# Expert tiles: two scatters in flight for neighbouring tiles of one expert, and the second projection two tiles late

## The reference, cut to what matters

```python
scores = xf @ gate_w.T + gate_b + bias                     # 2048 tokens, 8 experts
top_scores, top_idx = jax.lax.top_k(scores, 2)
gates = jax.nn.softmax(top_scores, axis=-1)
h = jax.nn.silu(einsum('td,ehd->teh', xf, w1) + b1)        # 512 -> 352
y = einsum('teh,edh->ted', h, w2) + b2                     # 352 -> 512
out = einsum('ted,te->td', y, comb)                        # comb: the two gates of each token
x = x + out
```

## Time and profile before

| what | value |
|---|---|
| three runs, median (lowest to highest) | 1113.1 us (1109.29 to 1113.27) |
| the profiled execution, its own time | 1108.39 us |
| its span in the profile | 1106.6 us |
| PE busy | 1024.7 us, 93% |
| DVE busy | 808.6 us, 73% |
| POOL busy | 377.5 us, 34% |
| stretch from the first to the last scatter instruction | 880.19 to 1098.41 us |

### The profile page before, as it was taken

One profiled execution on the slowest core, in us unless ns is written; L12 is line 12 of the kernel. 1 busy time (PEld: TensorE's weight loads), 2 busy tenths in 40 slices (PEclk: granted clock), 3 DMA queues, 4 the chain that ended last, 5 costly groups with the idle time before them and its releaser, 6 DMA issues.

```text
span 1106.6 us, 16870 instructions
## 1 busy us (share of the span) xinstructions
PE 1024.7 (93%) x4963; PEld 843.8 (76%) x4964; DVE 808.6 (73%) x1606; ACT 392.4 (35%) x825; POOL 377.5 (34%) x307
## 2 busy tenths in 40 slices
PE   4999899999999997999999999999959899899994
PEld 3888688888888875788888888888748777777773
DVE  6888876687676777789999989999898534443342
ACT  3345444444444554221221221221247533333331
POOL 2665554455454443200000000000047244444442
PEclk9999999999999999999999999999979999999998
DMA  6001620001000121521111111111335154455443
GB/s 238 1 0 38 233 72 20 20 20 37 19 20 20 58 76 57 201 67 38 47 47 47 47 38 38 47 47 38 114 103 202 35 89 88 92 95 91 88 88 55
DMA packets 45551, 76.72 MB, mean 69 GB/s; under 512 B 4072, under 2 KB 16400, under 8 KB 45392
## 3 DMA queue, kind: packets, MB, share of 16 engines
q1 hardware_dynamic: 36784, 55.88, 14.9%
q0 software_dynamic: 8736, 20.45, 10.3%
HBM read 52.99 MB, written 23.33 MB: 69 GB/s over the span
## 4 chain that ended last, share of the span: by engine, by line
PE 67%; DMA 15%; DVE 10%; issue 4%; ACT 2%; POOL 0%; POOLq 0%; SPq 0%; DVEq 0%; ACTq 0%
DMA out<-y,slot_token 13%; PE pK L1383 10%; PE pK L1385 10%; PE pK L1384 10%; PE pX L1383 5%; PE pX L1385 5%; PE pX L1384 5%; PE pA L1383 5%; PE pA L1385 5%; PE pA L1384 5%; PE pA L1497 2%; PE pT L1449 1%; DMA xg<-xn_dram,slot_token 1%; DVE gprod L1182 1%; DVE xn_lo L1018 1%
## 5 line engine op out<-in xcount | busy, mean ns | idle before, releaser
L855 ACT ACTIVATE q<-pK 128x512 f32<-128x512 f32 x64 | 38.3, 599 | 277.1 <-PE pK L1385 277.1
L559 POOL TENSOR_TENSOR kacc<-kacc,k_hi 128x512 f32 (+1 forms) x64 | 91.7, 1433 | 122.0 <-ACT k_hi L733 121.1
L635 POOL TENSOR_TENSOR xb<-x_in,bo_b 128x512 f32<-128x512 f32 x15 | 19.4, 1293 | 319.9 <-DVE x L1168 311.4
L563 POOL TENSOR_TENSOR kacc<-kacc,k_lo 128x512 f32 (+1 forms) x64 | 98.9, 1546 | 34.5 <-DVE k_lo L1040 25.9
L1383 PE MATMUL pA<-k_hi,xn_hi 128*128 128x512 f32 x256 | 101.1, 395 | 7.3 <-DVE k_lo L1040 7.3
L1383 PE MATMUL pX<-m_hi,qsT_hi 128*128 128x512 f32 x256 | 105.7, 413 | 0.0
L647 POOL DMA_INDIRECT out<-y,slot_token x39 | 66.8, 1712 | 113.8 <-DMA out<-y,slot_token 91.9
L1018 DVE TENSOR_TENSOR xn_lo<-xn,xn_hi 128x512 fp32r<-128x512 f32 x64 | 91.1, 1424 | 19.7 <-ACT xn_hi L726 19.7
L1383 PE MATMUL pK<-wq_hi,xnT_hi 128*128 128x512 f32 x256 | 100.9, 394 | 3.1 <-DVE wq_lo L1018 3.1
L1383 PE MATMUL pK<-wk_hi,xnT_hi 128*128 128x512 f32 (+1 forms) x256 | 102.1, 399 | 1.0 <-DVE xnT_lo L1018 1.0
L1384 PE MATMUL pK<-wq_lo,xnT_hi 128*128 128x512 f32 x256 | 100.7, 393 | 0.0
(11 more groups left out here) (232 smaller groups left out, 2460.1 us busy)
## 6 DMA issues: line engine op xcount, KB each, us to landing
w_in<-in_ffn_w SPq DMA_DIRECT2D x22, 256.0 KB, 3.2
w_in<-in_ffn_w SPq DMA_DIRECT2D x8, 704.0 KB, 7.7
xn<-in_attn_hidden_states SPq DMA_DIRECT2D x16, 256.0 KB, 5.8
wk_in<-in_attn_Wk SPq DMA_DIRECT2D x4, 1024.0 KB, 5.1
wv_in<-in_attn_Wv SPq DMA_DIRECT2D x16, 256.0 KB, 2.8
wo_in<-in_attn_Wo SPq DMA_DIRECT2D x16, 256.0 KB, 3.0
wk_in<-in_attn_Wq SPq DMA_DIRECT2D x4, 1024.0 KB, 5.1
xnT_dram<-xnT SPq DMA_DIRECT2D x4, 1024.0 KB, 12.9
```

The lines of the kernel that those rows point to most:

```text
L559: pool.tensor_tensor(acc, acc, f(k_hi[:, b * CW:(b + 1) * CW]), ALU.add).then_inc(pool_own, 1)
L563: pool.tensor_tensor(acc, acc, f(k_lo[:, b * CW:(b + 1) * CW]), ALU.add).then_inc(kacc_done, 1)
L635: pool.tensor_tensor(xb[:, :], x_in[:, :], bo_b[:, :], ALU.add).then_inc(xb_ready, 1)
L855: nc.scalar.activation(q[:, (c % 2) * CW:(c % 2 + 1) * CW], pK[:, (c % 2) * 512:(c % 2 + 1) * 512], ACT.Relu).then_inc(q_ready, 1)
```

## The change

`add_out(i)` now waits for the landing of add_out(i-2) always, and for that of add_out(i-1) only where tile i-1 belongs to another expert or where tile i is filled up entirely. Which it is stands in a new table `add_after`, which DVE works out after `tile_expert`; POOL loads one value of it into a register ahead of each scatter from the fourth on and waits with that. There is one landing semaphore for even and one for odd tiles. Two small POOL instructions put the constants of the table (`add_base`) in an earlier stage.

The second projection runs two tiles late instead of one: PE's loop is h(i), gT(i+1), y(i-2), hT(i). So `hT_hi` and `hT_lo` have two buffers each, DVE's order follows, and POOL gathers five tiles ahead of the scatter instead of three. The work per tile is the same.

```diff
             def add_out(i):
+                if i >= 3:
+                    other = pool.value_load(add_after[0:1, i - 1:i], min_val=16, max_val=16 * NS)
                 pool.wait_ge(y_ready, i + 1)
-                if i > 0:
-                    pool.wait_ge(s_add, 16 * i)
+                if i >= 2:
+                    pool.wait_ge(s_add[i % 2], 16 * (i // 2))
+                if i >= 3:
+                    pool.wait_ge(s_add[1 - i % 2], other)
+                elif i >= 1:
+                    pool.wait_ge(s_add[1 - i % 2], 16)
                 pool.indirect_dma_start(out, bass.IndirectOffsetOnAxis(slot_token[:, i:i + 1].bitcast(U32), 0),
-                                        y[:, i % 2 * D:(i % 2 + 1) * D], None, compute_op=ALU.add).then_inc(s_add, 16)
+                                        y[:, i % 2 * D:(i % 2 + 1) * D], None, compute_op=ALU.add).then_inc(s_add[i % 2], 16)
...
-            gather(2)
+            for i in range(2, 5):
+                gather(i)
             for i in range(NS):
-                if i + 3 < NS:
-                    gather(i + 3)
+                if i + 5 < NS:
+                    gather(i + 5)
                 add_out(i)
...
             link(v.tensor_scalar(tile_expert[:, :], padt[:, 0:TW], float(E - 1), None, ALU.min))
+            link(v.tensor_tensor(same[:, :], padt[:, 1:TW], padt[:, 0:NS], ALU.is_equal))
+            link(v.scalar_tensor_tensor(out=same[:, :], in0=padt[:, 1:TW], scalar=E - 0.5, in1=same[:, :],
+                                        op0=ALU.is_le, op1=ALU.mult))
+            link(v.scalar_tensor_tensor(out=add_after[:, :], in0=same[:, :], scalar=-16.0, in1=add_base[:, :],
+                                        op0=ALU.mult, op1=ALU.add))
...
-            def dve_y(i, b):
+            def dve_y(i, b, added):
                 dve.wait_ge(y_put, i + 1)
                 if not (isinstance(i, int) and i < 2):
-                    dve.wait_ge(s_add, 16 * i - 16)
+                    dve.wait_ge(s_add[b], added)
...
             with dve.Fori(2, NS // 2) as h:
                 for b in range(2):
                     dve_gT(2 * h + (b + 1))
-                    dve_y(2 * h + (b - 1), 1 - b)
-                    dve_hT(2 * h + b)
-            dve_y(NS - 2, 1)
-            dve_hT(NS - 1)
-            dve_y(NS - 1, 0)
+                    dve_y(2 * h + (b - 2), b, 16 * h - 16)
+                    dve_hT(2 * h + b, b)
+            dve_y(NS - 3, 0, 16 * (NS // 2) - 16)
+            dve_hT(NS - 1, 0)
+            dve_y(NS - 2, 1, 16 * (NS // 2) - 16)
+            dve_y(NS - 1, 0, 16 * (NS // 2))
...
             pe_hT(0)
             pe_h(1, first_experts[1])
             pe_gT(2, 0)
-            pe_y(0, first_experts[0])
             pe_hT(1)
             with pe.Fori(1, NS // 2) as h:
                 for b in range(2):
                     i = 2 * h + b
                     pe_h(i, expert(i))
                     pe_gT(2 * h + (b + 1), 1 - b)
-                    pe_y(2 * h + (b - 1), expert(2 * h + (b - 1)))
+                    pe_y(2 * h + (b - 2), b, expert(2 * h + (b - 2)))
                     pe_hT(i)
             pe_h(NS - 1, expert(NS - 1))
-            pe_y(NS - 2, expert(NS - 2))
+            pe_y(NS - 3, 0, expert(NS - 3))
             pe_hT(NS - 1)
-            pe_y(NS - 1, expert(NS - 1))
+            pe_y(NS - 2, 1, expert(NS - 2))
+            pe_y(NS - 1, 0, expert(NS - 1))
```

More of the change, by code:

```diff
@@ L187, in block_kernel @@
     table = sb("table", 3 * TW, R2 + 2944)
+    add_base = sb("add_base", NS, R2 + 3584)
+    same = sb("same", NS, R2 + 3744)
+    add_after = sb("add_after", NS, M0 + 6656, I32)
     padt = sb("padt", TW, R2 + 3424)
@@ L195, in block_kernel @@
     hT = sb("hT", HB * P, 188 * KB + 1408)
-    hT_hi = sb("hT_hi", HB * P, 190 * KB + 896, F32R)
-    hT_lo = sb("hT_lo", HB * P, 192 * KB + 384, F32R)
+    hT_hi = [sb("hT_hi0", HB * P, 190 * KB + 896, F32R), sb("hT_hi1", HB * P, M0 + 5120, F32R)]
+    hT_lo = [sb("hT_lo0", HB * P, 192 * KB + 384, F32R), sb("hT_lo1", HB * P, 193 * KB + 896, F32R)]
     xg = sb("xg", 2 * D, 196 * KB)
@@ L321, in block_kernel @@
         s_g = [sem(f"s_g{i}") for i in range(2)]
-        s_add = sem("s_add")
+        s_add = [sem(f"s_add{i}") for i in range(2)]
         gT_put = sem("gT_put")
@@ L529, in _ @@
                 load_w2(e)
-            sp.wait_ge(s_add, 16 * NS)
+            sp.wait_ge(s_add[0], 16 * (NS // 2 + 1))
+            sp.wait_ge(s_add[1], 16 * (NS // 2))
             sp.wait_ge(x2_stored, 16 * NT)
@@ L624, in _ @@
             pool.wait_ge(dump_stored, 32)
+            link(pool.iota(iota32[:, 0:TW], pattern=[[16, TW // 2], [0, 2]], base=16, channel_multiplier=0))
+            link(pool.tensor_copy(add_base[:, :], iota32[:, 0:NS]))
             link(pool.iota(iota_r32[:, :], pattern=[[1, P]], base=0, channel_multiplier=0))
@@ L1343, in dve_gT, with dve_hT @@
                 lo(gT_lo[:, :], pT[:, :], gT_hi[:, :]).then_inc(gT_lo_ready, 1)
-            def dve_hT(i):
+            def dve_hT(i, b):
                 dve.wait_ge(hT_ready, i + 1)
-                if not (isinstance(i, int) and i == 0):
-                    dve.wait_ge(y_put, i)
-                v.tensor_copy(hT_hi[:, :], hT[:, :]).then_inc(hT_hi_ready, 1)
+                if not (isinstance(i, int) and i < 2):
+                    dve.wait_ge(y_put, i - 1)
+                v.tensor_copy(hT_hi[b][:, :], hT[:, :]).then_inc(hT_hi_ready, 1)
                 dve.wait_ge(hT_hi_ready, i + 1)
-                lo(hT_lo[:, :], hT[:, :], hT_hi[:, :]).then_inc(hT_lo_ready, 1)
-            def dve_y(i, b):
+                lo(hT_lo[b][:, :], hT[:, :], hT_hi[b][:, :]).then_inc(hT_lo_ready, 1)
+            def dve_y(i, b, added):
                 dve.wait_ge(y_put, i + 1)
                 if not (isinstance(i, int) and i < 2):
-                    dve.wait_ge(s_add, 16 * i - 16)
+                    dve.wait_ge(s_add[b], added)
                 v.tensor_scalar(y[:, b * D:(b + 1) * D], pK[:, 512:1024], slot_gate[:, ds(i, 1)], None,
@@ L1361, in _ @@
             dve_gT(1)
-            dve_hT(0)
+            dve_hT(0, 0)
             dve_gT(2)
-            dve_y(0, 0)
-            dve_hT(1)
+            dve_hT(1, 1)
             for i in range(2, 4):
                 dve_gT(i + 1)
-                dve_y(i - 1, 1 - i % 2)
-                dve_hT(i)
+                dve_y(i - 2, i % 2, 0)
+                dve_hT(i, i % 2)
             with dve.Fori(2, NS // 2) as h:
@@ L1622, in pe_hT, with pe_y @@
                 last.then_inc(hT_put, 1)
-            def pe_y(i, e):
+            def pe_y(i, b, e):
                 pe.wait_ge(hT_lo_ready, i + 1)
@@ L1629, in pe_y @@
                     w = min(P, W2C - n * P)
-                    hs = (hT_hi[0:w, n * P:(n + 1) * P], hT_lo[0:w, n * P:(n + 1) * P])
+                    hs = (hT_hi[b][0:w, n * P:(n + 1) * P], hT_lo[b][0:w, n * P:(n + 1) * P])
                     at_ = e * (HB * D) + n * D
```

## The result

The changed kernel takes 1078.99 us in the median (1076.71 to 1081.43, 4 runs) against 1112.81 before (1109.29 to 1113.27, 4 runs). The ratio is 0.9704, 95% interval 0.9681 to 0.9728: 3.0% faster, with 33.8 us between the medians, as forecast (1082, range 1075 to 1098). The profiled execution has a span of 1079.3 us; the sum gave 1078.6.

What follows compares the result with a forecast made beforehand. One scatter's round trip (5.74 us a tile) was taken as the bound; at PE's 4.85 us h(38) starts at 1053.8, the last scatter at 1070.4, plus 8.2 gives 1078.6. Forecast 1082 us, range 1075 to 1098.

Steps and rivals of the forecast that it cites:

- What bounds the kernel: Expert stage: one scatter's round trip, 5.74 us per tile, sets the pace; afterwards PE does, at 4.85 us per tile.
- "Issue" on TensorE is a consequence of late gathers: Expert stage: PE's 20.0 us of "issue" are register loads exposed at waits for late gathers, and go with them.
- The gathers, five ahead: POOL's gathers issued five tiles ahead land with four microseconds of cover; PE's 13.1 us of waits go.
- The register load on POOL: POOL's cycle of scatter, gather and load makes 3.0 to 4.5 us, under 4.85, so the load counts as hidden.
- Borders: Seven pairs of tiles at an expert's border and the last two stay serial, scatters 5.7 us apart; PE feels nothing.
- The sum: All terms added up to the whole kernel's span: 1078.6 us, 28.0 less than before.
- the 0.71 us between y and its scatter: End of the stage: add_out(36) starts 0.71 us after DVE's y, at 1059.7, a figure taken from the earlier trace.
- A sign that I named and that did not come: Profile of the changed kernel: POOL's idle time after landings falls from 80 us to under 20.
- 1: Rival: PE's register loads stay exposed, 5.1 us a tile (1091 us) to 5.35 (1100 us); chance 12 in 100.
- 4: Rival: POOL's register load decides the cycle and makes the kernel slower, 1125 to 1130 us; chance 3 in 100.
- 2: Rival: transfers hinder each other or POOL's load is slow, 5.0 to 5.2 us a tile, 1087 to 1093; chance 8 in 100.
- Rival 3: The table allows no overlap, cycle stays 5.7 us, time 3.5 to 5 us over before; chance 4 in 100.

Runs made afterwards that it cites:

- e1: Changed kernel, but each scatter again waits for the landing of the one before, with no register load on POOL: 1112.44 us, ratio 1.0014 to the kernel before.
- e5: e2 with TensorE's register load for y moved ahead of the next tile's transposes: 1092.97 us, ratio 0.9849 to the kernel before the change.
- e3: e2 with gathers four instead of three ahead of the scatter, second projection still one tile late: 1080.86 us, ratio 0.9731 to the kernel before.
- e4: Changed kernel with gathers four instead of five ahead of the scatter, nothing else: 1103.50 us, ratio 0.9933 to the kernel before.
- e2: Kernel before plus only the table's wait; projection one tile late, gathers three ahead: 1099.87 us, ratio 0.9900 to the kernel before.

## Why the prediction was right, step by step

- *What bounds the kernel.* Right. e1 with the round trip kept takes the time of before; TensorE bounds what comes next, and the 4.82 and 4.81 us that I read from two undisturbed tiles were 4.78 over 35 tiles. The stage got 30.7 us shorter (222.6 to 191.9); the sum gave 28.0.
- *"Issue" on TensorE is a consequence of late gathers.* Right. e5 shows that the gaps are the register load behind the gather's wait, and with timely gathers 1.0 of the 20.0 us is left. e3 adds another cause that I had not seen: behind y's short wait for hT's split the next load is exposed too.
- *The gathers, five ahead.* Right. Tile 12's gather starts at 919.19 and lands after 4.2 us, and its transposes start at 927.65: 4.3 us of cover, where I gave four. e4 shows what this cover is worth.
- *The register load on POOL.* I bounded the cycle by 3.0 and 4.5 us. Between the scatters at 900.05 and 903.23 it is 3.18: the load leaves no gap, the idle time ahead of the scatter is the same 0.30 us as ahead of a gather. The row shows why: the first load, the one for that scatter, starts at 900.3, while the scatter ahead is still being issued (900.05 to 901.63), and takes the longest of all, 0.50 us. In the median a load takes 0.29. My sum for the cycle added it to the issues, and in the trace it runs beside them.

```profile
L651 POOLq TENSOR_LOAD <-add_after x36: 283/289/502, 900.3 to 1065.4; - x36
```

- *Borders.* The seven borders and the last two stand where forecast, and TensorE feels none: its steps from h(4) on are 4.75 to 4.80 us. I left out tiles 1 and 2, which wait for the scatter ahead by a constant: 5.8 and 5.9 us, hidden too.
- *The sum.* 1078.6 against 1079.3 is in part luck: it hides errors that cancel. The attention half took 3.2 us longer (the start itself came out: from the first transpose of `w_in` to h(3) are 75.6 us, before 75.4); the tile takes 4.78 instead of 4.85 us (2.5 us less); the last two intervals were 0.3 us longer together; and from h(38) to the first of the last three scatters it was 5.3 us instead of 5.9. The term that was off in these 5.9 is the 0.71 us between y and its scatter: in the earlier trace rows that scatter still waited for the landing ahead of it. Released by y it takes 0.28 us (917.01 to 917.29, and 921.67 to 921.95).
- *A sign that I named and that did not come:* idle time of POOL after landings under 20 us. The row says 61.1 us, of which 36.1 are put down wrongly, as said above. But the other 25.0 us are over 20 too: the seven borders make 19.3 and tiles 1 and 2, which I had left out, 5.7. By the time between the end of y and the start, 26 of 38 scatters are released by y (I gave 29), 11 by a landing, and that of tile 3 by POOL's own queue. The intervals were the better sign.
- *Rivals.* 1 and 4 did not come true. Of 2, transfers in each other's way, the trace now shows a case: the scatters of 900.05 and 903.23 were in flight together for 1.5 us and landed after 4.7 and 5.1 us, inside the 4.4 to 5.4 of the earlier trace rows, so nothing there cost time. Over all 39 the landing took 4.5, 4.9 and 5.2 us (least, median, most). I had put the time with two in flight at about one of 4.85 us; it is 0.3 us in the mean, as shown above. The Trainium skill's sentence that two concurrent DMAs serialize (SBUF — State Buffer, "Can I just issue two DMAs to hit both halves?") is not tested by this: at 0.60 busy the engines had room, and no run here fills them. Rival 3 is e1 by its effect, and its price (3.5 to 5 us over before) was a little high: the stage was 2.6 us longer, the median not distinguishable.

## What to carry to other kernels

When a wait for a transfer sets the step, look at what else stands behind the same instruction in its queue: here the wait alone gave 1.0% (e2), one gather more ahead of the scatters brought it to 2.7% (e3), and the gathers without the wait gave nothing (e1). A register load was free while its engine's sequencer ran ahead, and cost 0.3 to 0.4 us behind many of the waits at which the sequencer stood, so place it ahead of the wait. A step of software pipelining buys its slack (0.16 us a tile here, e3 against the change) with a tile at the end (4 us here), and with 39 tiles that was nearly an even trade.

## What the runs showed of the hardware that I had not expected

- TensorE's register load mostly takes 0.30 us, but up to 0.99 us in some cases before the change and 0.96 after it. In the change the long ones were hidden too: from h(3) to h(38) no "issue" gap of TensorE's weight loads is left.
- The profile put 27 scatters down to landings, and for 18 of them y was the releaser; several of those landings came later than the scatter that they should have released.
- The stretch ahead of h(3) varies by up to 5 us between the profiled executions (883.9 to 888.6 us). In the two of the changed kernel it makes 2.2 of the 2.3 us between their spans; whether it is most of the scatter of all runs is not shown.
